# Lookup comparisons shared between VectorE and GpSimd, lookups placed in other slots, four projection banks in batch 0

## What is computed

```python
x = x + xattn(layernorm(x), ctx)      # x (4, 512, 512), ctx (4, 512, 256)
x = x + ffn(layernorm(x))
# xattn: q = LN_head(x @ Wq + bq), k = LN_head(y @ Wk + bk), v = y @ Wv + bv   (16 heads of 32)
#   the last 16 context rows (DCA) have weights Wkv_dca and a softmax of their own; the two results are added
# ffn:   gate = x @ lut[gate_idx].T; up = x @ lut[up_idx].T     (1376 x 512 indices each)
#        out = (silu(gate) * up) @ lut[down_idx].T
```

## Time and profile before

| | |
|---|---|
| median of 3 runs | 919.49 us (918.78 to 923.66) |
| profiled execution | 919.11 us, its span 917.3 us |
| busy in the span | PE 804.1, DVE 521.6, ACT 487.0, POOL 237.1 us |
| batch 0 | 0 to about 245 us of the span |

### The profile page before, as it was taken

The page is one execution under the profiler, slowest core; times in us unless marked ns, Lnnn a source line. Parts: engine busy times, 40 slices in busy tenths (PEclk is TensorE's granted clock), DMA queues, the critical chain, the costliest instruction groups (busy, mean ns, idle before and its releaser), DMA issues.

```text
span 917.3 us, 15590 instructions
## 1 busy us (share of the span) xinstructions
PE 804.1 (88%) x5892; PEld 320.9 (35%) x5892; DVE 521.6 (57%) x934; ACT 487.0 (53%) x960; POOL 237.1 (26%) x280
## 2 busy tenths in 40 slices
PE   3683666599989999999999999999999999979998
PEld 1231222233345333332444333334443332234443
DVE  6847999788564798221646884216468940052220
ACT  2444677677534688565246885662468856521100
POOL 3764200000146322100463221003642210002330
PEclk9886788799999999999999999999999999998999
DMA  8327953244400000111100000101000000000001
GB/s 274 86 79 210 294 162 106 84 142 132 151 0 1 1 2 1 35 36 38 59 1 1 1 2 7 64 24 46 1 1 1 1 23 25 24 24 1 1 2 44
DMA packets 45167, 50.12 MB, mean 55 GB/s; under 512 B 6048, under 2 KB 33184, under 8 KB 45088
## 3 DMA queue, kind: packets, MB, share of 16 engines
q1 hardware_dynamic: 43536, 48.71, 17.8%
q10 hardware_dynamic: 1552, 0.37, 0.2%
HBM read 40.61 MB, written 8.45 MB: 53 GB/s over the span
## 4 chain that ended last, share of the span: by engine, by line
issue 32%; PE 31%; DVE 15%; POOL 14%; ACT 5%; DMA 1%; ACTq 1%; POOLq 0%; DVEq 0%
PE ps L1089 20%; POOL hrstd L497 7%; DVE arena L761 5%; DVE nmax L899 4%; PE ps L1279 3%; PE ps L1262 3%; POOL arena L462 3%; ACT ps L646 2%; PE ps L1235 2%; POOL arena L460 1%; POOL xrstd L467 1%; ACT arena L671 1%; PE ps L1135 1%; DMA wf_lo<-in_lut 1%; PE ps L1268 1%
## 5 line engine op out<-in xcount | busy, mean ns | idle before, releaser
L1089 PE MATMUL ps<-arena,wf_hi 128*128 128x512 f16 (+1 forms) x704 | 212.3, 384 | 4.6 <-DVE arena L814 1.7
L646 ACT ACTIVATE ps<-ps,nmax 128x496 f32<-128x496 f32 x256 | 165.2, 646 | 64.0 <-DVE arena L900 62.9
L671 ACT ACTIVATE arena<-ps 128x1024 f32<-128x1024 f32 x128 | 125.4, 1023 | 83.4 <-PE ps L1268 83.3
L899 DVE TENSOR_REDUCE nmax<-ps 128x2 f32<-128x992 f32 x128 | 151.5, 1184 | 22.4 <-PE ps L1235 22.3
L1089 PE MATMUL ps<-arena,wf_lo 128*128 128x512 f16 (+1 forms) x352 | 134.4, 382 | 0.0
L497 POOL TENSOR_TENSOR hrstd<-hvar,mhalf 128x16 f32<-128x16 f32 x32 | 94.5, 2953 | 132.1 <-DVE hvar L842 132.1
L1089 PE MATMUL ps<-wf_hi,arena 128*128 128x512 f16 (+1 forms) x352 | 114.1, 380 | 2.9 <-POOL arena L462 2.8
L1135 PE MATMUL ps<-arena,wf_lo 128*32 128x512 f16 (+1 forms) x1056 | 76.7, 433 | 27.3 <-ACT wf_lo L575 26.4
L1089 PEld LDWEIGHTS ps<-arena,wf_hi 128*128 128x128 f16 (+1 forms) x704 | 66.7, 101 | 93.4 <-DVE arena L768 11.0
L761 DVE TENSOR_SCALAR arena<-arena,wf_lo 128x2048 f16<-128x2048 f16 (+1 forms) x132 | 90.4, 746 | 5.8 <-PE ps L1135 2.8
L467 POOL TENSOR_TENSOR xrstd<-xvar,mhalf 128x1 f32<-128x1 f32 x32 | 18.1, 565 | 262.7 <-DVE xvar L797 262.6
(11 more groups left out here) (133 smaller groups left out, 1026.6 us busy)
## 6 DMA issues: line engine op xcount, KB each, us to landing
arena<-idx SPq DMA_DIRECT2D x124, 128.0 KB, 2.7
arena<-in_x SPq DMA_DIRECT2D x32, 256.0 KB, 2.8
wf_lo<-in_idx SPq DMA_DIRECT2D x10, 512.0 KB, 6.6
out<-arena SPq DMA_DIRECT2D x16, 256.0 KB, 2.0
idx<-wf_hi SPq DMA_DIRECT2D x10, 384.0 KB, 4.4
wf_lo<-in_idx SPq DMA_DIRECT2D x11, 256.0 KB, 7.0
arena<-in_ctxT SPq DMA_DIRECT2D x4, 512.0 KB, 4.9
arena<-in_Wq SPq DMA_DIRECT2D x4, 256.0 KB, 5.4
```

The source lines that it names most:

```text
L646: last = act.activation(sc, sc, ACT.Exp, bias=nmax[:, 0, t, h:h + 1], accum_out=den[:, 0, t, h:h + 1])
L671: act.activation(probs[n_ % 2][:, 2 * p:2 * p + 2, :], ps[:, bank:bank + 2, :], ACT.Exp).then_inc(s["probs_set"], 1)
L899: dve.tensor_reduce(nmax[:, 0, t, 2 * p:2 * p + 2], sc[:, :, DCA:S], AX_X, ALU.max, negate=True)
L1089: last = pe.matmul(dst, l, r, start=(first and i == 0), stop=(stop and i == len(todo) - 1))
```

## The change

- One of the four comparisons of each chunk (q = 3) is an instruction of GpSimd instead of VectorE. It waits for the load of the chunk and for all products of the chunk before it; TensorE waits for it before its last eight products, SP before it loads the buffer again.
- The lookups stand in other slots: 11 instead of 16 in the first half (every third pair of slots has none), one at S_SHIFT + 1 instead of S_SHIFT, 21 instead of 16 in the second half, two of them in each of the slots n = 1, 4, 7, 10, 13.
- Batch 0 projects into four banks in turn, so `project(u)` waits for `normalise(u - 4)`; GpSimd's `rstd(u)` then waits for `normalise(u - 2)`. In every batch VectorE does `variance(u + 1)` ahead of `normalise(u)`.
- GpSimd centres the key weights (before: VectorE), takes `values_low` one slot earlier, `lookup_constants` in slot 3 instead of at the start, and its casts at other slots. VectorE sums the key weights at the start. ScalarE copies the value weights ahead of the last two query weights.
- Twelve small DMAs (norm weights, biases, the table) are issued by SP behind the big loads, not by ScalarE.
- A logarithm of one column is put ahead of the real one, before its wait for the sums.

```diff
-LOOKUP_SLOT = {slot: c for c, slot in enumerate(
-    [S_ONE + 2 * i + 1 for i in range(NQ)] + [S_SHIFT] + [S_TWO + n_ for n_ in range(G * T)])}
-assert len(LOOKUP_SLOT) == NCH
+LOOKUPS = {S_ONE + 2 * i + 1: 1 for i in range(NQ) if i % 3 != 1}
+LOOKUPS.update({S_SHIFT + 1: 1})
+LOOKUPS.update({S_TWO + n_: 1 + (n_ % 3 == 1) for n_ in range(G * T)})
+LOOKUP_FROM = {slot: sum(c for o, c in LOOKUPS.items() if o < slot) for slot in LOOKUPS}
+assert sum(LOOKUPS.values()) == NCH
+
+
+CONVERT_AT = {it: S_ONE + max(0, 3 * (it - EARLY - 2)) for it in range(EARLY, IT)}
+
+
+def lookups_in(slot):
+
+    return range(LOOKUP_FROM[slot], LOOKUP_FROM[slot] + LOOKUPS[slot]) if slot in LOOKUPS else ()
...
-        LB0 = (FB, FB + 1, VB, VB + 1)
+        LB0 = (VB, VB + 1, TB, TB + 1)
         ps16 = lambda bank: ps[:, bank, :].bitcast(F16)
         pair_bank = lambda m: SC + 2 * (m % 3)
-        proj_bank = lambda u: AB + (u + 1) % 2
+        proj_bank = lambda u, first: AB + (u % 4 if first else (u + 1) % 2)
...
-                    sp.wait_ge(s["oh_set"], NJ * (c - 1))
+                    sp.wait_ge(s["oh_set"], (NJ - 1) * (c - 1))
+                    sp.wait_ge(s["oh_pool"], c - 1)
...
+            for i, name in enumerate(("qn_w", "qn_b", "kn_w", "kn_b", "kn_dca_w", "kn_dca_b")):
+                sp.dma_start(st_ln[:, i, :], row(name, 0, HD).to_broadcast([P, HD])).then_inc(s["ln_in"], 16)
+            sp.dma_start(bvm, A["bv"]).then_inc(s["bv_in"], 16)
+            sp.dma_start(bvd, A["bvd"]).then_inc(s["bv_in"], 16)
+            for r in range(NR4):
+                sp.dma_start(lut_w[r * 32:(r + 1) * 32, :], row("lut", r * NJ, (r + 1) * NJ).to_broadcast([32, NJ])).then_inc(s["lut_in"], 16)
...
+            def keys_centred():
+                key = st_kv[0].rearrange("p (h d) -> p h d", d=HD)
+                pool.wait_ge(s["wk_sum"], 1)
+                link(pool.tensor_scalar(sum_k, sum_k, -1.0 / HD, 0.0, ALU.mult, ALU.add))
+                pool.tensor_tensor(key, key, sum_k.unsqueeze(2).to_broadcast([P, KC * H, HD]), ALU.add).then_inc(s["wk_cent"], 1)
...
+            def one_hot(c):
+                lo, hi = CHUNKS[c]
+                n_ = NR4 * (hi - lo)
+                pool.wait_ge(s[f"rep_in{c % 2}"], 16 * NR4 * (c // 2 + 1))
+                if c == 0:
+                    pool.wait_ge(s["j_set"], 1)
+                    pool.wait_ge(s["ps1"], T)
+                else:
+                    pool.wait_ge(s["oh_used"], NJ * c)
+                pool.tensor_scalar(l_oh[NJ - 1][:, 0:n_], l_rep[c % 2][:, 0:n_], l_j[:, NJ - 1:NJ], None, ALU.is_equal)\
+                    .then_inc(s["oh_pool"], 1)
...
+                    if u >= 2:
+                        pool.wait_ge(s["qn_set"], nth(a, NU, u - 1))
...
-            lookup_constants()
+            keys_centred()
             norm(1, 2, (0, 0))
             norm(1, 3, (0, 0))
 
             def prepare(slot):
-                if slot == 1:
+                if slot == 0:
                     values_low()
                 if slot == 2:
                     shift_patterns()
-                if 3 <= slot < 3 + EARLY:
-                    convert(slot - 3)
-                if S_ONE <= slot < S_ONE + IT - EARLY:
-                    convert(EARLY + slot - S_ONE)
+                if slot == 3:
+                    lookup_constants()
+                if 4 <= slot < 4 + EARLY:
+                    convert(slot - 4)
+                for it in range(EARLY, IT):
+                    if slot == CONVERT_AT[it]:
+                        convert(it)
+                for c in lookups_in(slot):
+                    one_hot(c)
...
+                act.wait_ge(s["S_exp"], nth(a, NS, NS))
+                act.activation(warm[:, :], sqs[0][:, 0, HD:SQ], ACT.Ln)
                 act.wait_ge(s["den_set"], nth(a, T, T))
-                act.wait_ge(s["S_exp"], nth(a, NS, NS))
...
+            act.wait_ge(s["wv_in"], 16)
+            act.activation(fl(wv[0]), st_kv[1], ACT.Copy, scale=WS).then_inc(s["wv_hi"], 1)
...
-                if LOOKUP_SLOT.get(slot, 0):
-                    lookup_out(LOOKUP_SLOT[slot] - 1)
+                for c in lookups_in(slot):
+                    if c:
+                        lookup_out(c - 1)
...
-                for q in range(NJ):
+                for q in range(NJ - 1):
...
                 for u in range(NU + 1):
-                    if 1 <= u < NU:
-                        normalise(a, u)
                     if 1 <= u < NU - 1:
                         variance(a, u + 1)
+                    if 1 <= u < NU:
+                        normalise(a, u, prev is None)
                     if u:
...
-            normalise(first, 0)
             variance(first, 1)
+            normalise(first, 0, True)
...
-                    pe.wait_ge(s["oh_set"], NJ * c + q + 1)
+                    pe.wait_ge(*((s["oh_set"], (NJ - 1) * c + q + 1) if q < NJ - 1 else (s["oh_pool"], c + 1)))
...
+                    if prev is None:
+                        if u >= 4:
+                            pe.wait_ge(s["qn_set"], nth(a, NU, u - 3))
+                    elif u >= 2:
                         pe.wait_ge(s["qn_set"], nth(a, NU, u - 1))
-                    elif u == 1 and prev is not None:
+                    elif u == 1:
...
-            core((0, 0), lambda slot: look_up(LOOKUP_SLOT[slot] - 1) if LOOKUP_SLOT.get(slot, 0) else None, (0, 1), None)
+
+            def prepare(slot):
+                for c in lookups_in(slot):
+                    if c:
+                        look_up(c - 1)
+
+            core((0, 0), prepare, (0, 1), None)
             look_up(NCH - 1)
```

66 lines of the change are left out of this document (28 added, 38 removed).

## The result

| | before | after |
|---|---|---|
| median | 920.33 us (918.78 to 923.66, 4 runs) | 1053.97 us (1048.79 to 1056.89, 4 runs) |
| ratio | | 1.144, 95% interval 1.138 to 1.150 |
| span of the profiled execution | 917.3 us | 1047.0 us |
| mean granted clock | 0.961 | 0.901 |

The change makes the kernel 14.4% slower. The forecast was 931.1 us, with a range of 916 to 945.

The account below looks back on a forecast made before the run. Bounds: VectorE in batch 0's first score half, TensorE in the second and from 240 us, a chain in the projections. +0.5 - 5 + 0 + 15.5 + 1 + 0 = +12 on 919.11 gives 931.1 us, range 916 to 945.

Parts of the forecast that it names:

- the duration of GpSimd's comparison: Compare of 128x2048 f16 on GpSimd: 1.9 us from the one-input rows, upper end 4.2 us from the two-input row.
- The rival of a slow comparison: GpSimd's comparison takes 4.2 us, delaying VectorE in the first half and TensorE in the second: 970 us, chance 0.10.
- the first, a mean near 1.9 to 2.1 us: Sign expected in the profile: the comparison on GpSimd has a mean duration near 1.9 to 2.1 us.
- the three under "I am wrong if": First half under 70 us, doubled slots costing under 2 us each, or scores beginning before 74 us.
- The port: First half: GpSimd and VectorE exclude each other by instruction, PSUM maxima untouched; 9.8 us lost, some 0.6 for chunk 0.
- First half: First score half of batch 0: 15.4 us less without conflict, -5 with port losses, up to +3.6 at low clock.
- Between the halves: Transposes some 2.5 us earlier, but a lookup of 1.9 to 2.6 us behind them: 0, from -3 to +1.
- Second half: Five more lookups on full TensorE, +15.5 us (+9.2 to +22); last chunk compared after its load, +1 (0 to 3).
- just in time: Second half: GpSimd's compare ends 1.9 us after the first products; TensorE asks for it after 2.6, or 3.3 in single slots.
- Projections: Batch 0's projections: first key projection near 49.4 us, chain through GpSimd's queue; +0.5 us, from -7 to +3.
- the queue doesn't run 7 us ahead: Rival in the projections: GpSimd's queue without a gap, last key power 7 us earlier, 913.2 us in all; chance 0.11.
- Batches 1 to 3: Later batches: `normalise` waits a little longer, next power some 1 us earlier; 0, from -2 to +2 us.

Follow-up runs that it names:

- experiment 6: The changed kernel with GpSimd's comparison cut to the first 704 of 2048 columns, the rest of the fourth comparison left out: 945.4 us.
- experiment 1: The changed kernel with the fourth comparison back on VectorE, all other edits kept: 933.2 us.
- 9: The changed kernel with a quick multiply-add instruction on the same 2048 columns in place of GpSimd's comparison (fourth comparison left out): 956.9 us.
- experiment 10: Four comparisons on VectorE, other edits kept, with x tiles 2 and 3 loaded at chunks 18 and 22, not 22 and 25: 926.5 us for 933.2.

## Why the prediction was wrong

**The step that failed** is the duration of GpSimd's comparison: "The one-input rows give 621 ns for 512 and 1049 for 1024, 0.84 ns an element more, so 1.9 us". It took 5.87 us at the median, 5.4 alone. The rows were right; they are of a multiply-add, a kind that I took for "one input". The upper end, 4.2 us from the two-input row, was too low as well, so the range could not hold the time. It is not the only step: with an instruction of the assumed length the time is 956.9 us, 26 above the forecast and still outside its range, and that part lies in the second half (below). (The Trainium skill's GPSIMD Engine Reference, "Elementwise", by which I had estimated 3.07 us, is also short of the 5.4 measured.) The rival of a slow comparison had the right mechanism and the wrong price, 970 us: it counted single losses at VectorE and single waits of TensorE, and left out that at over 5 us GpSimd and VectorE need 7.5 us a chunk at the port alone, that TensorE and the reload of the buffer wait in the same ring, and that TensorE's granted clock was lower there (0.74 for 0.97). Of the signs set out beforehand the first, a mean near 1.9 to 2.1 us, told the failure at once; the three under "I am wrong if" did not occur, for each looked for a change that costs less than forecast.

**The port** works between the comparisons as the forecast said, instruction by instruction with the waiting one next, and maxima and copies from PSUM are free of it. Its price in the first half can be read with the quick instruction: 82.1 against 76.1 us with four comparisons on VectorE, which is 6.0 lost and the saving of 10 x 0.66 with it, 12.6 us (forecast 9.8 + 0.6); with the 704 columns of experiment 6 the same sum gives 0.8 + 6.6 = 7.4.

**First half.** With that instruction -2.8 us (84.9 to 82.1) for -5 forecast. With the whole GpSimd part undone it is -8.8, that is the five lookups moved out of it, and the forecast's own terms give the same: 15.4 less 10 x 0.66.

**Between the halves**, forecast 0: -2.7 in experiment 1 and -1.7 in 9; +2.4 in the changed kernel. The forecast's term also has the lookup behind the transposes, which my marks put into the second half. Before, the scores follow the transposes of 175.73 at once; in experiment 1 a lookup stands between:

```profile
176.25 1.47 PE L1262 MATMUL ps<-arena 32*128 32x512 f16 x12
```

```profile
162.82 0.59 PE L1288 MATMUL ps<-ident_h,caug 128*128 128x128 f16 x4 [7.88 <-DVE caug L961]
163.33 3.60 PE L1170 MATMUL ps<-arena,wf_lo 128*32 128x512 f16 x32
166.87 1.29 PE L1300 MATMUL ps<-arena 32*128 32x512 f16 x12
```

It takes 3.54 us from start to start (1.9 to 2.6 forecast), so the term measured the forecast's way is -2.7 + 3.5 = +0.8, within -3 to +1.

**Second half**, forecast +15.5 and +1: +27.2 us in experiment 1 already (3.5 of them the lookup just named), and +40.9 with the quick instruction. A doubled slot does cost what the forecast said, and its five waits for ScalarE's copies came as forecast, 5.9 us in experiment 1. These two starts of scores and the wait show it, 6.79 us for 3.70:

```profile
171.38 0.83 PE L1300 MATMUL ps<-arena 32*128 32x512 f16 x12 [1.17 <-ACT arena L709]
...
176.33 1.91 PE L1170 MATMUL ps<-arena,wf_lo 128*32 128x512 f16 x32 [1.18 <-ACT wf_lo L612]
...
178.17 0.83 PE L1300 MATMUL ps<-arena 32*128 32x512 f16 x12
```

5 x 3.09 is the 15.5. Missing was what is keyed to chunks and not to slots: the loads of x, 6.7 us of the second half (96.1 to 89.4 in experiment 10). With the 3.5 of the lookup these make 25.7 of the 27.2 us; a wait of TensorE for ScalarE at 171.38, 1.2 us, is most of the rest. The reloads of chunks come late too (VectorE waits 9.4 us for them in the second half of experiment 1, and 2.7 before), but by experiment 10 they hardly reach TensorE. Further 13.7 us go to GpSimd's instruction, which I had called just in time. TensorE hardly waits for its result (1.3 us there). What it costs goes through VectorE, whose comparisons stand behind it at the port: TensorE's waits for them grow from 7.1 to 15.0 us, and its own work takes 4.2 us more (85.2 for 81.0) at a granted clock of 0.92 for 0.96.

**Projections**, forecast +0.5: the first scores are 1.4 us earlier. The first key projection starts at 48.58 (about 49.4 forecast), the last key power at 68.23 against 70.09, where I had 71.2. It was right that the queue doesn't run 7 us ahead.

**Batches 1 to 3**, forecast 0: from the last lookup on 675.4 us against 672.7.

**The sum, with the right place for each error** (the change's span less that before, 129.7, each from one profiled execution): 13.6 for all but GpSimd's comparison (experiment 1's span of 930.9), 24.6 for an instruction of 2.0 to 2.5 us there (955.5), 91.5 for its being 5.7 (1047.0). The forecast had +12 for the first two together, which are 38.2.

## What to carry to other kernels

Before a step is moved to another engine, look for a row of that very instruction there, with the same operations and operands; if there is none, the range has to hold a price of a few times the nearest row. A comparison on GpSimd did not run beside VectorE's comparisons: its whole duration counted against them, while reductions and copies from PSUM went on. So add up, for each chunk, what the two engines need one after the other. And when work is packed closer, list what is keyed to its count: prefetches came late then, 6.7 us here, and to see whether a late load matters, look at the engine that bounds the stage.
